# Moving the row normalisations of x ahead of the projection blocks in an eight-core attention and feed-forward layer

## The reference

```python
x = x + _layernorm(attn(_layernorm(x), q_heads, k_heads, v_heads, output_proj))
x = x + _layernorm(ffn(_layernorm(x), W1, b1, W2, b2))
# attn: 16 heads of 64, causal softmax over 8192 positions, then output_proj
# ffn: relu(x @ Wq1.T + b1) @ Wq2.T + b2
```

## Time and profile before

| | us |
|---|---|
| Median of the runs (2) | 4032.24 |
| The profiled execution, its own time | 4027.23 |
| Its span, core 0 (the slowest) | 4025.7 |
| Spans of all cores | 3973.9 to 4025.7 |
| PE busy, core 0 | 2628.5 (65%) |
| ACT busy | 1463.1 (36%) |
| DVE busy | 766.0 (19%) |
| POOL busy | 538.9 (13%) |
| Mean granted TensorE clock, cores 0 to 3 and 4 to 7 | 0.781 and 0.806 |

### The profile page before, as it was taken

One profiled execution on the slowest core, in us unless ns is written; L12 is line 12 of the kernel. 1 busy time (PEld: TensorE's weight loads), 2 busy tenths in 40 slices (PEclk: granted clock), 3 DMA queues, 4 the chain that ended last, 5 costly groups with the idle time before them and its releaser, 6 DMA issues.

```text
span 4025.7 us, 41257 instructions; the slowest of 8 cores (3973.9 to 4025.7 us)
## 1 busy us (share of the span) xinstructions
PE 2628.5 (65%) x10022; PEld 871.2 (22%) x10122; DVE 766.0 (19%) x1292; ACT 1463.1 (36%) x2401; POOL 538.9 (13%) x1428
## 2 busy tenths in 40 slices
PE   1226765555775757775777776777777767676673
PEld 0112222222231212221221121111122222222221
DVE  2320111111001231113112223222200031213121
ACT  1122121221224436663766653666666710000000
POOL 0000111111112221112012222211100010000000
PEclk9667778888895567777877876677687769999997
DMA  5343444443323313332334442444322223333334
GB/s 162 90 129 89 104 126 118 122 123 108 102 73 104 87 48 98 91 96 62 98 96 105 117 110 73 107 117 111 103 54 49 49 65 106 97 110 105 89 104 137
DMA packets 439381, 395.86 MB, mean 98 GB/s; under 512 B 308593, under 2 KB 308593, under 8 KB 439154
## 3 DMA queue, kind: packets, MB, share of 16 engines
q1 hardware_dynamic: 371058, 248.22, 25.7%
q10 hardware_dynamic: 48384, 88.10, 6.8%
q0 software_dynamic: 19712, 56.91, 4.3%
HBM read 277.51 MB, written 84.15 MB: 90 GB/s over the span
## 4 chain that ended last, share of the span: by engine, by line
PE 38%; DMA 25%; ACT 16%; issue 9%; DVE 5%; POOL 3%; SPq 1%; ACTq 1%; DVEq 0%; POOLq 0%
PE oa_ps L680 14%; ACT expT_sb L658 11%; PE sc_ps L639 8%; DMA kfm<-kevac_sb 7%; DMA ln1b<-lno_sb 4%; DMA w2t_sb<-wq 4%; PE oa_ps L805 4%; PE sc_ps L561 3%; DMA w1t_sb<-wq 3%; PE op_ps L715 3%; PE sc_ps L827 2%; POOL expT_sb L667 2%; DMA wq<-qp_sb 1%; PE sc_ps L397 1%; PE sc_ps L374 1%
## 5 line engine op out<-in xcount | busy, mean ns | idle before, releaser
L680 PE MATMUL oa_ps<-expT_sb,vband_sb 128*65 128x512 bf16 (+13 forms) x2560 | 881.2, 419 | 409.3 <-ACT expT_sb L658 218.8
L658 ACT ACTIVATE expT_sb<-sc_ps 128x1024 bf16<-128x1024 f32 x864 | 859.5, 1022 | 417.2 <-PE sc_ps L639 400.9
L639 PE MATMUL sc_ps<-qu_sb,kband_sb 64*128 64x512 bf16 (+13 forms) x2560 | 524.9, 420 | 76.7 <-DVE lntmp_sb L768 42.4
L543 PE MATMUL sc_ps<-fm_sb,wA_sb 128*128 128x512 bf16 x1004 | 274.5, 426 | 272.6 <-ACT kevac_sb L548 235.7
L680 PEld LDWEIGHTS oa_ps<-expT_sb,vband_sb 128*65 128x65 bf16 x2560 | 239.6, 122 | 858.3 <-issue 830.4
L667 POOL TENSOR_TENSOR expT_sb<-expT_sb,dmask_sb 128x32 bf16<-128x32 bf16 x1024 | 244.6, 253 | 741.6 <-ACT expT_sb L658 543.9
L805 PE MATMUL oa_ps<-fm_sb,w1t_sb 128*128 128x512 bf16 x1003 | 257.4, 404 | 130.8 <-DMA w1t_sb<-wq 71.9
L652 ACT ACTIVATE expT_sb<-sc_ps 128x416 bf16<-128x416 f32 (+12 forms) x832 | 250.1, 356 | 249.1 <-PE sc_ps L639 236.4
L561 PE MATMUL sc_ps<-wB_sb,fm_sb 128*128 128x512 bf16 x1003 | 250.7, 405 | 45.3 <-ACT vstage_sb L567 43.7
L639 PEld LDWEIGHTS sc_ps<-qu_sb,kband_sb 64*128 64x128 bf16 x2560 | 130.7, 97 | 596.6 <-issue 577.3
L853 ACT ACTIVATE rstd_sb<-aggr_sb,eps_sb 128x1 f32<-128x1 f32 x16 | 4.7, 294 | 686.8 <-DVE aggr_sb L851 686.8
(11 more groups left out here) (79 smaller groups left out, 1683.8 us busy)
## 6 DMA issues: line engine op xcount, KB each, us to landing
vband_sb<-vtm SPq DMA_DIRECT2D x160, 260.0 KB, 4.4
kband_sb<-kfm SPq DMA_DIRECT2D x160, 256.0 KB, 3.3
xb_sb<-x_batch SPq DMA_DIRECT2D x64, 512.0 KB, 5.4
qscr_sb<-w1T ACTq DMA_DIRECT2D x128, 256.0 KB, 4.4
qscr_sb<-w2T ACTq DMA_DIRECT2D x128, 256.0 KB, 4.3
w1t_sb<-wq SPq DMA_DIRECT2D x128, 256.0 KB, 2.7
w2t_sb<-wq SPq DMA_DIRECT2D x128, 256.0 KB, 2.6
vtm<-vstage_sb POOLq DMA_DIRECT2D x64, 260.0 KB, 2.4
```

What stands on the lines that cost most here:

```text
L543: O("tensor", lambda e, kc=kc, dc=dc, fs=fs, pa=pa: e.matmul(pa, wA_sb[:, dc * 1024 + kc * 128: dc * 1024 + (kc + 1) * 128], fm_sb[:, (fs ...
L639: sl=sl, qoff=qoff: e.matmul(sc_ps[:, ss * 512 + qoff:(ss + 1) * 512], kband_sb[64 * h2: 64 * h2 + 64, sl * 1024 + (kb % 8) * 128: sl * 10 ...
L658: O("scalar", lambda e, up=up: e.activation(expT_sb[:, up * 1024:(up + 1) * 1024], sc_ps[:, up * 1024:(up + 1) * 1024], AF.Exp, scale=0.12 ...
L680: sp=(kb == nkb - 1): e.matmul(oa_ps[0:65, h2 * 512 + qoff:(h2 + 1) * 512], vband_sb[:, sl * 1040 + (kb % 8) * 130 + h2 * 65: sl * 1040 + ...
```

## The change

In the loop of the Q stage, `ln1o_group(tt+2)` and `ln1b_group(tt)` are called ahead of block tt's matmuls and evacuations in place of behind them; `q_transposes(tt+2)` stays behind. In the loop of the K and V stage, `ln1b_group(tt+4)` is called ahead of block tt; `kv_transposes(tt+2)` stays behind. No instruction is added or taken away.

```diff
         for tt in range(TT):
             fs = (tt % 2) * 8
+            if tt + 2 < TT:
+                ln1o_group(tt + 2)
+            ln1b_group(tt)
             for qc in range(8):
...
             if tt + 2 < TT:
-                ln1o_group(tt + 2)
                 q_transposes(tt + 2)
-            ln1b_group(tt)
...
         for tt in range(S // 512):
             fs = (tt % 2) * 8
+            if tt + 4 < S // 512:
+                ln1b_group(tt + 4)
             for kc in range(8):
...
-            if tt + 4 < S // 512:
-                ln1b_group(tt + 4)
             if tt + 2 < S // 512:
                 kv_transposes(tt + 2)
```

## The result

| | us |
|---|---|
| Changed kernel, median of 11 runs | 4095.6 (4066.35 to 4136.44) |
| Kernel before, median of 10 runs | 3996.16 (3980.34 to 4045.63) |
| Ratio | 1.0223, 95% interval 1.0177 to 1.0268 |
| Profiled execution of the changed kernel, its span (core 5) | 4095.6, 4094.1 |

The change makes the kernel 2.2% slower, by the ratio 89 us (71 to 107) on a kernel before of 3996 us, by the medians 99 us. Medians and ranges are over all runs and the ratio over the fast ones alone, since in three runs of the changed kernel (4122 to 4136 us) the cores of one die were slowed. Both runs of before that stood ahead of the prediction were among its longer ones, so that 36 of the 65 us between 4161 and 4095.6 are the base (4032 against 3996); the other 29 are the sum.

The account below looks back on a forecast made before the run. TensorE waiting for ACT was taken to bound the K and V stage. K and V +139 us and Q -10 took the profiled 4027.2 to 4156 us; 5.0 for the median gave 4161, range 4105 to 4215.

Parts of the forecast that it names:

- rival (a): K and V: x loads still arrive while ACT evacuates, later stretches stay 16.1 us; +6 us, 4038 us; chance 0.05.
- the stretch on ACT between two blocks: K and V: ACT's time between V evacuations and next K evacuation becomes 30.5 us in place of 16.1.
- the lead: K and V boundary: TensorE ends V on average 1.5 us before ACT ends its evacuations, subtracted from 32.0 us.
- the chain: K and V boundary: eight transposes, x load, four tiles, then K evacuation; 32.0 us from first transpose, spread 30 to 34.
- The block: K and V: each of twelve blocks between stretches takes 35.5 us in place of 38.5.
- The first block: K and V start: first evacuation waits for group 4 and comes at 438.2 us, 32.2 us late.
- The Q stage: Q stage: casts of the next weights begin at 260.6 us instead of 270.81, -10 us.
- The sign that this length should not change: After K and V block 12's start: the length from there to the end should be the same.
- TensorE's idle time that ACT ends: K projection in the K and V stage: this idle time should grow from 209 us by some 160.
- Rival (b): K and V: blocks shrink as waits grow; 31.5 us blocks give 4113 us, 27.6 about 4066; chance 0.03.
- (c): K and V: dearer, block stays 38.5 us or chain takes 36; 4197 to 4209 us, together 4245; chance 0.17.
- (d): SyncE's queue: transposes drain as fast as the skill's 261 GB/s, giving 4085 us; chance 0.02.

Follow-up runs that it names:

- e3: Changed kernel with two of each group's four x loads issued ahead of the transposes: 4008.79 us, ratio 1.0040 to the kernel before.
- e6: Changed kernel with each set of eight transposes for K and V blocks 2 to 15 issued twice: 4195.67 us.
- e7: Kernel before with each set of eight transposes for K and V blocks 2 to 15 issued twice: 4028.52 us.
- e1: Kernel before with only the K and V edit, Q stage as before: 4095.15 us, ratio 1.0281.
- e2: Kernel before with only the Q edit, K and V stage as before: 3981.43 us, ratio 0.9971.
- e8: Kernel before with K stores tracked as eight buffers and V stores as four, so none waits for the one ahead: 3920.58 us, ratio 0.9807.
- e9: Kernel before plus Q edit, tiles spread inside K and V blocks, two x loads ahead of transposes, free stores, more staging slots: 3645.09 us, ratio 0.9120.
- e5: Kernel before with each group's first two x loads issued by ACT between K and V evacuations: 4030.42 us, ratio 1.0104.

## Why the prediction was right or wrong

**The mechanism** was right but for one detail, the moment at which the transposes may start (below): the loss lies in K and V, SP's order of transposes and x loads behind TensorE's last V matmuls sets it, ACT's evacuations queue behind the group, and rival (a) did not come about. Queue place (e3), doubled transposes (e6, e7) and the split edits (e1, e2) each moved the time as this says, the latter two within 12 us of their expectations.

**The size** was too large, and the step that failed is the stretch on ACT between two blocks. On the path up to block 12's start the prediction had 1190 us (1199.7 less the 10 of the Q stage); the profiled core has 1154.0. The terms:

- The stretch, "32.0 - 1.5 = 30.5 us", measured 27.5: 11 x 3.0 = 33 us too much. Of each 3.0 us, 1.6 are the lead, taken as 1.5 us (the twelve boundaries of before average 1.65): I let the transposes wait for "TensorE's last V matmul", but each waits for its own chunk, and over the eleven boundaries (590.35 us is the one shown) they start on average 3.1 us ahead of the end of ACT's evacuations. The other 1.4 are the chain: 30.6 us on average, not 32.0. In the Q stage, where I had read it the second time, four tiles took 15.0 us; here 13.5 to 13.9 (607.22 to 620.73 is one). The trace shows why: the four stores of a group write one tracked buffer, so that the fourth waits for the third to land. There the third landed after 4.5 us (208.01 to 212.48), beside the next group's x loads; here, with those behind the transposes, after 2.1 us (617.37 to 619.42). The first time, four tiles took 13.6 us in the Q stage too, and the first x load was slower (7.9 us from its issue to Ln, here 6.6 on average).
- The block, "35.5, near the clean row", measured 34.6: 10 us too much for twelve.
- The first block: 435.2 against 428.2 computed on this core, 7 us too little. Core 5 is the latest here: by the eight cores the first evacuation came between 415 and 435 us, on average at 423.0.
- The Q stage, -10 us, measured -10.3 in the profile and -12 us in the run of that edit alone.

33 + 10 - 7 = 36 us, which is the distance at block 12. Averaged over the cores, block 12 starts 78 us later than before, where the prediction had 129.

Behind block 12 the changed profile took 2940 us and the one of before 2965, with the same order. This is the base and no effect of the change: in the profiled execution of before only cores 0 and 1 took 2965 us, at a mean granted clock of 0.77 to 0.78 from block 12 on; its other six cores took 2923 to 2940 us at 0.80 to 0.81, and the eight of the changed kernel 2925 to 2945 us at 0.79 to 0.81. The sign that this length should not change thus held. The 36 us, these 25 and the 5 added for the median make up the distance of 65 us between 4161 and 4095.6.

Against the range, 4105 to 4215: the chain (30.6 us) and the block (34.6 us) lie inside the spreads that I gave them, 30 to 34 and 34.0 to 36.5. The lead had no spread at all, and the base had none: I had worked from one profiled execution near the upper end of what this kernel takes and did not widen the lower end for it. On a base of 4032 us the ratio gives 4122, inside the range; the median is 4095.6 because the base is 3996. Of the other signs, TensorE's idle time that ACT ends grew by 98 us (208.8 to 306.7), not by 160.

**Rival (b)**, blocks that shrink as the waits grow, was real with a smaller size: it said that the blocks must come down to 31.5 us for less than 2% with stretches of 30.5 us, and they came to 34.6. The reason given for it (kevac waits for K stores) was the right one, as e8 shows. (c) and (d) did not occur: eight transposes still took 10.0 us to issue with no K store and no x load in flight (590.35 us above). The Trainium skill's 261 GB/s for DMA transposes (DMA: Bandwidth & Descriptors, "Latency and other measured facts") is not reached here: 1.05 MB in 10.0 us are 105 GB/s.

The K and V edit alone came out no faster than the whole change (1.0281 against 1.0223), and the intervals overlap, so that the ratios can't show the Q edit's 12 us. The traces can in part: averaged over the cores, the first K evacuation comes at 433.0 us with the K and V edit alone and at 423.0 with both, and block 12 starts at 1145.5 and 1139.7. Beyond block 12 the difference between the two ratios stays open.

## What to carry to other kernels

Moving a step ahead of the work it was meant to hide behind is only a gain if its inputs are there: look, on the queue that fetches them, at what stands in front of them and what that waits for. The order on one engine can look the same (groups and evacuations by turns) and still be one step further on against another queue. And a chain that fills the gaps between blocks was better cut into pieces inside the block (92 us faster) than moved from one end of it to the other (89 us slower); then look for the next bound, since here freeing the stores was worth 77 us by itself and 150 us once the tiles were cut up and more staging slots were there.

## What the runs showed of the hardware that I had not expected

The block of the changed kernel hardly depends on TensorE's clock. Core 5 ran its first eleven blocks at a granted clock of 0.73 to 0.78, core 0 at 0.86 to 0.94 after the same stops; on average over twelve blocks they took 34.6 and 34.3 us. Block 3, at 620.73 us on core 5 and at 604.78 on core 0:

```profile
620.73:654.27 33.54, 32.48 (x117) 12.91 (x118) 0.00 (x0) 9.29 (x16) 5.94 (x11) 0.77 0.19 68
```

```profile
604.78:639.27 34.49, 30.13 (x123) 12.65 (x126) 0.00 (x0) 9.21 (x16) 5.95 (x11) 0.90 0.21 69
```

At the lower clock the matmuls are busy longer and the block is no longer. That the stores set its pace is seen where the clock is the same: block 13 of the kernel before ran at 1.00, the upper level of 2.4 GHz, and took 35.32 us.

```profile
1096.06:1131.38 35.32, 28.59 (x127) 12.03 (x129) 0.00 (x0) 9.28 (x16) 6.48 (x12) 1.00 0.33 90
```

Block 13 of e9, also at 1.00 but with free stores and more staging slots, took 27.60 us (above). With no long stop left, e9 has that clock in both blocks shown, also while DMA is busy at 0.86.

And two x loads of 512 KB cost no less beside V than beside K (e5): averaged over the eight cores, the K part gained 2.7 us a block when they were moved off it (21.8 to 19.1), and the V part lost 4.0 (16.6 to 20.6).
